# A six-layer graph network on one core: adjacency tiles shared between two successive products, weights applied behind the aggregation

## The reference

```python
deg = clip(sum(adj, axis=1, keepdims=True), 1.0)
x = _layernorm(x + x @ W_self + (adj @ x / deg) @ W_neigh)
x = _layernorm(x + relu(adj @ (x @ L1_kernel) + L1_bias))
h = relu(adj @ (x @ W1) + b1)
h = relu(adj @ (h @ W2) + b2)
x = _layernorm(x + h)
x1 = swish((adj @ x) @ L3_W + L3_b)
x2 = swish((adj @ x1) @ L3_W + L3_b)
x = _layernorm(x + x2)
```

## Time and profile before

| | us |
|---|---|
| three runs: median (lowest to highest) | 1182.28 (1181.62 to 1182.28) |
| span of the profiled execution | 1180.8 |
| TensorE busy in it | 1161.3 |
| VectorE busy | 1043.4 |
| ScalarE busy | 822.2 |
| read from memory, MB | 365.36 |

### The profile page before, as it was taken

One profiled execution on the slowest core, in us unless ns is written; L12 is line 12 of the kernel. 1 busy time (PEld: TensorE's weight loads), 2 busy tenths in 40 slices (PEclk: granted clock), 3 DMA queues, 4 the chain that ended last, 5 costly groups with the idle time before them and its releaser, 6 DMA issues.

```text
span 1180.8 us, 18560 instructions
## 1 busy us (share of the span) xinstructions
PE 1161.3 (98%) x5056; PEld 898.0 (76%) x5056; DVE 1043.4 (88%) x1260; ACT 822.2 (70%) x1014; POOL 84.4 (7%) x72
## 2 busy tenths in 40 slices
PE   7999999999999999999999999999999999999996
PEld 3555555678888888888888888877888888888885
DVE  6999999988898889888888989999988899899896
ACT  1232222368878878778777888898877888878884
POOL 0000100001011000000000010010000000001101
PEclk9999999999999999999999999999999999999998
DMA  9988888788889978999987999998999988899992
GB/s 347 343 271 307 290 301 290 270 294 297 326 312 333 329 243 305 363 339 331 347 301 269 343 323 328 330 325 295 353 334 346 328 312 314 290 323 341 329 329 111
DMA packets 106945, 367.92 MB, mean 312 GB/s; under 512 B 11808, under 2 KB 16800, under 8 KB 106912
## 3 DMA queue, kind: packets, MB, share of 16 engines
q1 hardware_dynamic: 100096, 362.85, 85.5%
q10 hardware_dynamic: 6816, 4.66, 1.3%
HBM read 365.36 MB, written 2.10 MB: 311 GB/s over the span
## 4 chain that ended last, share of the span: by engine, by line
PE 92%; DVE 4%; DMA 1%; issue 1%; ACT 1%; POOL 0%; SPq 0%; DVEq 0%; POOLq 0%; ACTq 0%
PE agg L315 25%; PE agg L307 25%; PE agg L308 25%; PE agg L297 12%; PE p_gen L288 2%; DVE adj_lo L538 2%; DMA kept<-adj_tiles 1%; DVE deg_part L533 1%; PE p_mix L328 1%; PE p_turn L339 1%; PE p_mix L346 1%; PE p_rows L329 1%; PE p_rows L334 1%; ACT t_x L443 0%; DVE op_lo L522 0%
## 5 line engine op out<-in xcount | busy, mean ns | idle before, releaser
L538 DVE TENSOR_TENSOR adj_lo<-ring,adj_hi 128x1024 fp32r<-128x1024 f32 x584 | 692.6, 1219 | 40.3 <-ACT adj_hi L417 24.5
L417 ACT CAST adj_hi<-ring 128x1024 fp32r<-128x1024 f32 x584 | 603.3, 1054 | 149.5 <-PE agg L315 97.4
L307 PE MATMUL agg<-adj_hi,op_hi 128*128 128x512 f32 x1344 | 543.0, 404 | 0.8 <-ACT adj_hi L417 0.5
L308 PE MATMUL agg<-adj_hi,op_lo 128*128 128x512 f32 x1344 | 524.4, 390 | 0.0
L315 PE MATMUL agg<-adj_lo,op_hi 128*128 128x512 f32 x1344 | 416.5, 391 | 0.8 <-DVE adj_lo L538 0.8
L307 PEld LDWEIGHTS agg<-adj_hi,op_hi 128*128 128x128 f32 x1344 | 252.6, 188 | 59.3 <-issue 6.6
L315 PEld LDWEIGHTS agg<-adj_lo,op_hi 128*128 128x128 f32 x1344 | 250.7, 188 | 59.2 <-DVE adj_lo L538 6.5
L308 PEld LDWEIGHTS agg<-adj_hi,op_lo 128*128 128x128 f32 x1344 | 252.9, 188 | 54.6 <-issue 6.0
L297 PE MATMUL agg<-ring,hidden 128*128 128x512 f32 x352 | 160.8, 600 | 5.5 <-DMA ring<-adj_tiles 5.5
L533 DVE TENSOR_TENSOR deg_part<-deg_part,ring 128x1024 f32<-128x1024 f32 x104 | 126.8, 1219 | 5.4 <-DMA ring<-adj_tiles 3.3
L297 PEld LDWEIGHTS agg<-ring,hidden 128*128 128x128 f32 x352 | 65.7, 193 | 71.6 <-issue 69.8
(11 more groups left out here) (60 smaller groups left out, 418.5 us busy)
## 6 DMA issues: line engine op xcount, KB each, us to landing
ring<-adj_tiles SPq DMA_DIRECT2D x672, 512.0 KB, 5.3
kept<-adj_tiles SPq DMA_DIRECT2D x8, 1024.0 KB, 7.9
hidden<-x_blocks SPq DMA_DIRECT2D x8, 256.0 KB, 9.8
xT<-x_t ACTq DMA_DIRECT2D x8, 256.0 KB, 2.9
out<-t_x ACTq DMA_DIRECT2D x8, 256.0 KB, 6.1
w<-W ACTq DMA_DIRECT2D x2, 64.0 KB, 9.0
w_self<-W_self ACTq DMA_DIRECT2D x1, 64.0 KB, 6.2
w_neigh<-W_neigh ACTq DMA_DIRECT2D x1, 64.0 KB, 6.9
```

The source lines that it names most:

```text
L307: nc.tensor.matmul(bank_of(c), op_hi[:, j * D:(j + 1) * D], a_hi, start=(j == 0), stop=False)
L308: nc.tensor.matmul(bank_of(c), op_lo[:, j * D:(j + 1) * D], a_hi, start=False, stop=False)
L417: nc.scalar.copy(adj_hi[:, split_place(p, t), :], raw_tile(c, t)).then_inc(hi_ready, 1)
L538: nc.vector.tensor_tensor(adj_lo[:, s, :], raw_tile(c, t), adj_hi[:, s, :].bitcast(fp32), ALU.subtract).then_inc(vec_tile if p else first_ ...
```

## The change

The new kernel computes the same, with the same tiles, in another order. It is one straight program made from a table of steps. A step is one tile. The tables name blocks of 512 x 512 (two tiles): `(i, q, e)` is the block of destination chunk i and source chunk q, both counted in the order of the sweep. Even passes sweep the chunks 0 to 7, odd passes 7 to 0 (`chunk`).

- **Blocks used twice.** Where e is true, the two split tiles of the block are used for this pass (`finish`) and at once for the next pass too (`early`), whose operand for the source chunk q is ready by then, since q is done before i. The early products add up in a bank of their own (`e_acc`); ScalarE stores the sum of a chunk (`part`, L442) and VectorE adds it to the finished sum in the next pass (L529). Such are 25 blocks in each of the passes 0 to 4. They need not be loaded and split again, so passes 1 to 5 have 39 blocks instead of 64.
- **Steps.** In all 518 tiles are loaded (688 before), 440 are split (672 before), 78 are multiplied in float32 (96 before), and split products are made 440 times for the pass at hand and 250 times for the next. A pass from 1 to 5 has 78 steps, called step 0 to 77 of the pass here. Its chunks are finished with steps 9, 11, 15, 25, 35, 47, 61 and 77. Steps 0 to 19 have no second use; in passes 1 to 4 most of those behind them have, in pass 5 none.
- **Weights behind the sum.** Every pass aggregates the plain operand, with rows on the partitions of the finished result, and multiplies the finished sum by its weight (`times_weight`, L346: four 128-column products for each of 48 chunks). `gen` and the transposes are gone. In pass 0 x times (W_self + identity) takes four more products to a chunk (L320).
- **Post work.** VectorE takes the sum out of PSUM (L529, L531; in pass 0 ScalarE, L434), adds the bias (L555), applies relu and the residual (L562), makes statistics, moments and variance plus epsilon (L519), and normalises in passes 1, 3 and 5 (L583). GpSimd keeps the power alone. These stand at fixed steps behind the end of a chunk: the sum 5 steps behind it, the bias up to the variance 7, the normalising 8 (9 in pass 5, where the statistics stand at 8), the operand's low part 9. ScalarE's parts stand 6 to 10 behind.
- **Buffers.** `kept`, `hidden` and `xT` give way to two operands, seven slots for raw tiles and seven for split ones (four before).

The diff, cut to its core:

```diff
+    NEXT_ORDER = (
+        [(1, 1, False), (2, 1, False), (2, 2, False), (3, 3, False), (0, 0, False), (1, 0, False), (4, 4, False),
+         (2, 0, False), (5, 5, False), (5, 6, False)]
+        + [(3, q, True) for q in range(3)] + [(5, 7, False)]
...
+        + [(7, q, True) for q in range(7)]
+    )
...
+            def early(g, p, i, q, h):
...
+                    nc.tensor.matmul(e_acc[:], op_block(op_hi, p + 1, j), a_hi, start=first and b == 0, stop=False)
+                    nc.tensor.matmul(e_acc[:], op_block(op_lo, p + 1, j), a_hi, start=False, stop=False)
+                    last = nc.tensor.matmul(e_acc[:], op_block(op_hi, p + 1, j), a_lo, start=False,
+                                            stop=EARLY_TO[n] == g and b == BPT - 1)
...
+                for v, (i, q, e) in enumerate(order(p)):
+                    for h in range(2):
+                        finish(g + h, p, i, q, h, STEPS[g + h][5])
+                    if due is not None:
+                        times_weight(due)
+                        due = None
...
+                    if FINISHED_AT[p * CHUNKS + i] == g + 1:
+                        due = p * CHUNKS + i
...
+        AGG_AT = 5
+        BIAS_AT = 7
+        NORM_AT = 8
+        OP_AT = 9
...
+                    nc.vector.tensor_tensor(t_agg[:, n % 2, :], acc, cols(part, c), ALU.add).then_inc(agg_out, 1)
...
+                if p in (1, 3) and at == BIAS_AT:
+                    dve.wait_ge(zb_ready, n - CHUNKS + 1)
...
+                    moments_of(n)
...
-            with pool.Fori(0, len(NORM_PASSES) * CHUNKS) as n:
-                pool.wait_ge(moments_ready, BPC * (n + 1))
-                pool.nop(nofuse=True)
-                nc.gpsimd.tensor_scalar(var_eps[:], moments[:, :, 1], EPS, None, ALU.add).then_inc(var_ready, 1)
-                pool.wait_ge(var_ready, n + 1)
+            for m in range(len(NORM) * CHUNKS):
+                pool.wait_ge(var_ready, m + 1)
```

More of the change, by code:

```diff
@@ new lines, in chunk @@
+    def chunk(p, i):
+        return i if p % 2 == 0 else CHUNKS - 1 - i
+    STEPS = [(p, i, q, h, e, p == 0 and not e) for p in range(PASSES) for i, q, e in order(p) for h in range(2)]
+    TOTAL = len(STEPS)
+    FINISHED_AT = {}
+    BEGUN_AT = {}
+    EARLY_FROM = {}
+    EARLY_TO = {}
+    SPLIT_NO = {}
+    EARLY_NO = {}
+    for g, (p, i, q, h, e, whole) in enumerate(STEPS):
+        n = p * CHUNKS + i
+        FINISHED_AT[n] = g
+        BEGUN_AT.setdefault(n, g)
+        if e:
+            EARLY_TO[n] = g
+            EARLY_FROM.setdefault(n, g)
+            EARLY_NO[g] = len(EARLY_NO)
+        if not whole:
+            SPLIT_NO[g] = len(SPLIT_NO)
```

876 lines of the change are left out of this document (425 added, 451 removed).

## The result

The changed kernel took 1209.26 us, the median of four runs (1207.79 to 1212.07), against 1182.03 us for the kernel before (four runs, 1181.62 to 1182.28): a ratio of 1.0233, with a 95% interval of 1.0219 to 1.0248. The direction was forecast, the size was not: 1191 was said, with 1168 to 1208 as the range, and the result lies 1.3 us above its upper end. The profiled run took 1212.07 us with a span of 1210.2, so the terms of the forecast are held against 1210.2, where they had given 1189.3.

A forecast was written before the change was run, and what follows sets the result against it. TensorE was taken to set the time, with VectorE close behind. 1180.8 - 21.3 - 1.3 (tail) + 8.4 + 5.7 + 10.8 + 4.2 + 2 gave a 1189.3 span, forecast 1191 us, range 1168 to 1208.

The forecast's parts named there:

- TensorE's work: TensorE over the whole kernel: float32 tiles -31.0, split products +24.5, small products -14.8, in all -21.3 us.
- The start: Before the first chunk's end: x on ScalarE's queue and VectorE's wait for weights cost 0 us, bounds -2 and +5.
- the rivals, at 0.07: Pass 0 or the start: both upper bounds reached, giving 1200 us or more, up to 1215; chance 0.07.
- Pass 0: ScalarE's copy of sums out of PSUM, behind casts waiting for tiles, delays chunks: +2 us, bounds 0 and +6.
- Passes 1 and 3: TensorE waits for VectorE's sum near step 17: 8.4 us in pass 1, 5.7 in pass 3.
- Passes 2 and 4: no wait: Up to the third chunk's sum in passes 2 and 4, VectorE needs 10.4 us, below TensorE's 12.7: no wait.
- Pass 5: The last pass, without second use: VectorE is the bound and TensorE ends 10.8 us later.
- VectorE at 95% in pass 5: Sign that the forecast is right: VectorE busy over 95% in pass 5.
- The clock: Half clock behind TensorE's long waits: 2.1 us each in passes 1 and 3, 4.2 in all, none in pass 5.
- The ring: Rival: tiles landing late hold up VectorE's back-to-back adj_lo in passes 1, 3 and 5, +11, giving 1202 us; chance 0.20.
- Half the wait: Rival: passes 1, 3 and 5 lose the 0.9 power wait, normalising takes 0.4, clock holds: 1174 us; chance 0.17.
- VectorE keeps up: Rival: a chunk's post work fits in TensorE's slack and all waits vanish, giving 1162 us; chance 0.11.

The follow-up runs named there:

- E12: Changed kernel with E5's start, E6's copy, E4's later normalising, E3's earlier sums in passes 1 to 4, and pass 5's store one step later still: 1169.5 us.
- E5: Changed kernel with x and weight transfers reordered, W_self on its own semaphore, and VectorE and TensorE waiting for weights later: 1197.26 us.
- E6: Changed kernel with ScalarE taking pass 0's chunk sums out of PSUM 3 steps behind a chunk's end instead of 6: 1204.36 us.
- E3: Changed kernel with VectorE's sum 3 steps behind a chunk's end instead of 5: 1201.25 us.
- E9: Changed kernel with only ScalarE's store in pass 5 issued one step later: 1205.05 us.
- E4: Changed kernel with normalising and all that follows it one step later in passes 1, 3 and 5: 1191.22 us.

## Why the prediction missed, step by step

**TensorE's work: right, and hidden at first.** The forecast was -21.3 us. The busy time fell by 9.6 only, since work done at 1.2 GHz is counted as busy (the stretch 231 to 234 above is busy for 3.00 of 3.00 us at clock 0.50), and so, as I take it, are short waits inside a group of matmuls. In E12, with most waits gone, it is 1140.1 against 1161.3: -21.2. The test written into the prediction ("wrong, if the busy time does not fall by about 21") would have condemned a term that was right.

**The start: the step that failed most.** "I take 0 (bounds -2 and +5)" measured 11.9. The text had named both pieces, x on ScalarE's queue and VectorE's wait at its fifth tile, but priced them by the GB/s of the start and not by following the queue: six blocks of x stood behind x transposed and ten weights, and VectorE's wait for all ten weights stopped the ring. Those two things together are a wait, not a share of bandwidth: 10.82 us in one piece, with the half clock behind it. E5 recovers all of it with the same bytes. The case had stood among the rivals, at 0.07.

**Pass 0: right place, size short.** ScalarE's late copy was named and given 2 us (bounds 0 and 6); it lost 6.5. The two gaps are 2.6 of it. What was left out is the clock: each was followed by 3.4 us at half clock, 1.7 us of time, so that they cost more than twice their length (E6).

**Passes 1 and 3: right.** The waits are 8.19 and 6.52 us, for 8.4 and 5.7; with clock and small waits 12.8 and 8.5 for 10.5 and 7.8. In pass 3 the 0.8 more is what two normalisings of 1.03 instead of 0.6 come to. The reasoning, VectorE's tiles counted against TensorE's up to the third chunk's sum, holds. "Passes 2 and 4: no wait" was off by 1.6 and 2.3: the sum stands in VectorE's order behind adj_lo that come later than the margin of 12.7 to 10.4 had let me think, and E3 takes both to 181.5.

**Pass 5: right mechanism, terms short.** VectorE is the bound as said, with one gap per chunk. 10.8 was forecast and 17.0 lost. The wait for the power came as priced (0.90, though its bounds had been 0 and 1.9, so the digit is luck); residual, statistics, moments and variance took 2.12 per chunk (1106.11 to 1108.23) for 2.35. Normalising took 1.03 us per chunk to the next start (1110.35 to 1111.38) and not 0.6, which is 2.6 for six chunks. The choice "nearer to the middle, since the work per column lies between" was wrong: the row of four 128-column statistics (0.87) was a lower bound, not an upper one. On this the hint from the Trainium skill, VectorE: DVE Perf Modes ("The perf-mode tier table"), pointed the wrong way too; its table is for 2048 elements, and no doubled rate shows in 1.03 us for four instructions on 128 columns, where one addition on 512 columns takes 0.61. The wait for a cast (0.45 behind most chunks, 3.4 in all) had no term at all: the change makes ScalarE wait for VectorE's normalising before it may store, and behind the store stand the casts that VectorE wants next. E9 takes 3.5 off by moving it. These two make 6.1 of the 6.2 that were missing; against the 1.4 that the statistics block was priced too high, as much stays unassigned.

**VectorE at 95% in pass 5: not by the page.** It is busy for 116.2 of 131.5 us, 88%; the rest is its waits of 0.90 and 0.45 and its idle time behind the last tile. A bound that is a chain through three engines does not show as an engine at 95%.

**The clock: right where charged, too narrow.** The stretch behind the gap of passes 1 and 3 ran at 0.50, for 5.5 and 3.5 us, which is 2.7 and 1.8 us of time for the 2.1 charged in each. Not charged were two such stretches in pass 0 and the one behind the wait of the start. One of 3.4 us in pass 5 was not charged either, with the reason that VectorE is the bound there; no run tests that reason by itself.

**The rivals.** The ring did not run dry: tiles land in 4.5 us (the median over the whole program), less than the 5.4 from which it would decide, and none of the long waits of TensorE or VectorE behind the start is for a tile, even where VectorE takes them back to back; only ScalarE's copy in pass 0 stood behind casts that waited for tiles. Its number, 1202, was nearer than the forecast, but by chance. "Half the wait" and "VectorE keeps up" are refuted by the changed kernel's own trace, though E4 shows that the first was one step of a table away.

## What to carry to other kernels

Follow each queue at the start of the program transfer by transfer, up to the first thing that each engine waits for; a semaphore shared by ten transfers makes its first user wait for the last. A step that waits for another engine (a power, a shift, a store) belongs far enough down the in-order stream that the answer is there, and so does everything that waits for that step on the other engines: moves of this kind, with the same work on every engine, were worth 40 us here and turned 2.3% slower into 1.1% faster. Using a tile twice paid here by the work that it spared the engine which was short of time in that stage, and not by TensorE's.
